# Residual, normalisation, router, routing and scatter of a two-block network: one loop that routes two chunks at a time

## The reference

```python
x = x + _L0_conv_ref(_ln_c(x), ...)     # ends in relu(bn(out) + identity)
t = _to_tokens(x)                       # 6272 tokens of 256 channels
t = t + _L0_ffn_ref(_ln_t(t), router_w, expert_weights)

def _L0_ffn_ref(x, router_w, expert_weights):
    logits = jnp.einsum('bsh,eh->bse', x, router_w)
    rw = jax.nn.softmax(logits, axis=-1).reshape(T, E)
    vals, idx = jax.lax.top_k(rw, TOP_K)            # 2 of 32 experts
    w_masked = jnp.zeros_like(rw).at[jnp.arange(T)[:, None], idx].set(vals)
    def body(acc, we):
        w_e, W_e = we
        return (acc + x_flat * w_e[:, None] @ W_e, None)   # W_e is 256 x 256
```

## Time and profile before

| | us |
|---|---|
| median of 3 runs | 2848.42 |
| lowest and highest | 2834.99, 2849.97 |
| the profiled execution | 2840.76 |
| its span | 2838.9 |

### The profile page before, as it was taken

How to read it: one execution, slowest core, us unless ns; L and a number is a source line. 1 busy time by engine, 2 the same in 40 slices (tenths; PEclk the granted TensorE clock), 3 DMA queues, 4 the chain that set the end, 5 groups by cost and what they waited for, 6 DMA issues and landing times. The chain is left out here.

```text
span 2838.9 us, 36666 instructions
## 1 busy us (share of the span) xinstructions
PE 2048.5 (72%) x12037; PEld 1095.3 (39%) x12038; DVE 1423.7 (50%) x1980; ACT 1257.6 (44%) x1519; POOL 975.0 (34%) x721
## 2 busy tenths in 40 slices
PE   2999279996967300087655578289989999898998
PEld 1454145553535200066522245134434444343444
DVE  3666325553545750022245445358576675856753
ACT  1444112222545100021111134287878888788887
POOL 4332211110000027700076400155555555554554
PEclk9999669997988655599956689699999999999999
DMA  1100122210046144355522111355546555555554
GB/s 27 34 24 12 38 66 60 62 45 5 1 147 221 58 154 127 110 169 172 152 71 64 45 52 68 88 136 145 137 123 161 136 148 143 144 141 133 153 145 114
DMA packets 230098, 286.27 MB, mean 101 GB/s; under 512 B 50612, under 2 KB 186628, under 8 KB 229828
## 3 DMA queue, kind: packets, MB, share of 16 engines
q1 hardware_dynamic: 191268, 233.00, 30.2%
q0 software_dynamic: 12288, 25.72, 3.0%
q10 hardware_dynamic: 26400, 25.70, 2.6%
HBM read 209.00 MB, written 75.25 MB: 100 GB/s over the span
## 5 line engine op out<-in xcount | busy, mean ns | idle before, releaser
L2062 ACT ACTIVATE BIG<-psA,b_s 128x1024 f32<-128x1024 f32 x784 | 811.1, 1115 | 226.3 <-PE psA L2006 226.3
L2006 PE MATMUL psA<-x_r,w_r 128*128 128x512 f32 x1568 | 482.6, 430 | 45.1 <-ACT BIG L2062 28.1
L1995 POOL TENSOR_TENSOR BIG<-BIG 128x1024 f32<-128x1024 f32 x147 | 366.8, 2495 | 381.9 <-DVE BIG L2083 187.3
L2083 DVE SCALAR_TENSOR_TENSOR BIG<-psY,b_s,BIG 128x512 f32<-128x512 f32 x392 | 288.8, 746 | 302.2 <-PE psY L2016 276.9
L2016 PE MATMUL psY<-BIG,w_s 128*32 128x512 f32 x3136 | 396.4, 619 | 10.8 <-DVE BIG L2099 6.5
L2006 PEld LDWEIGHTS psA<-x_r,w_r 128*128 128x128 f32 x1568 | 273.8, 192 | 310.5 <-ACT BIG L2062 227.1
L1405 POOL DMA_INDIRECT gath<-yg_d,idx x128 | 133.3, 1042 | 269.3 <-DVE idx L1416 225.1
L1370 ACT ACTIVATE xv<-ps 128x512 f32<-128x512 f32 x66 | 39.4, 597 | 419.3 <-PE ps L1348 419.3
L1348 PE MATMUL ps<-ident,xv 128*128 128x128 f32 x264 | 40.4, 277 | 224.2 <-DMA xv<-xg_d 224.2
L1316 POOL DMA_INDIRECT xg_d<-xnb,idx x128 | 122.5, 957 | 129.5 <-issue 125.6
L2016 PEld LDWEIGHTS psY<-BIG,w_s 128*32 128x32 f32 x3136 | 81.8, 111 | 216.4 <-issue 130.2
(11 more groups left out here) (341 smaller groups left out, 3097.0 us busy)
## 6 DMA issues: line engine op xcount, KB each, us to landing
BIG<-wt_d SPq DMA_DIRECT2D x784, 128.0 KB, 2.8
xv<-hs_d SPq DMA_DIRECT2D x196, 128.0 KB, 3.1
xg_d<-zeros SPq DMA_DIRECT2D x64, 264.0 KB, 3.7
xv<-xg_d SPq DMA_DIRECT2D x66, 256.0 KB, 3.0
BIG<-ypad_d SPq DMA_DIRECT2D x288, 56.0 KB
xv<-x SPq DMA_DIRECT2D x64, 196.0 KB, 3.1
yg_d<-ex ACTq DMA_DIRECT2D x33, 256.0 KB, 3.3
yg_d<-sq ACTq DMA_DIRECT2D x33, 256.0 KB, 3.3
```

The costliest lines, as they stand in the source:

```text
L1995: eng.tensor_tensor(gacc[:, w % 2], gacc[:, w % 2], gsum[:, a % 2], ALU.add).then_inc(Q["acc"], 1)
L2006: mm = eng.matmul(psA[m % 3][:, b * BLK:(b + 1) * BLK], w1_r[:, m % 16], x_r[:, w % 2, b * BLK:(b + 1) * BLK], start=True, stop=True)
L2062: eng.activation(hid[:, m % 8], psA[m % 3][:], ACT.Gelu, bias=b1_s[:, m % 16:m % 16 + 1]).then_inc(Q["gel"], 1)
L2083: eng.scalar_tensor_tensor(out=dst, in0=psY[use % 2][:], scalar=b2_s[:, g % 4:g % 4 + 1], in1=wb[:, g % 3, b * BLK:(b + 1) * BLK], op0=ALU ...
```

## The change

Setup, loop, routing and scatter become one block. Its loop is written out in full and has 18 slots: 16 chunks and two more (`T + GC`), where `GC` = 2 chunks are a group. In slot s the engines do residual and normalisation of chunk s and transposes and router of chunk s-1; from slot 2 on, an even slot also finds the best two experts for the group before (`best`, `second_best`), and an odd slot gives its rows out (`grow`, `place`, `slots`). Instead of counting all tokens first, tiles are given to experts as the chunks go by: a state `st` of 32 experts (tokens so far, tiles so far, an offset) is updated a group, and new tiles are numbered behind those of earlier groups. Ranks within a group come from matmuls with `before_r` and `ones_r`; small matmuls spread tile counts and rows over the partitions. GpSimd scatters straight from `xnb`, now five buffers, as soon as the slot numbers of the group stand. `xn_d` goes. The zeros for `xg_d` are written by SyncE in the third convolution step, 64 transfers from a part of `ex` that GpSimd fills in the kernel's first block. The expert weights are loaded by SyncE, one transfer an expert, as the columns of `BIG` come free. `EID` is made at the end by one matmul from the table `owned`.

```diff
@@ third convolution step @@
+                @block.sync
+                def _(eng):
+                    eng.wait_ge(s_zero, 1)
+                    for q in range(ZQ):
+                        eng.dma_start(xg_d.ap().rearrange("r c -> (r c)").rearrange("(q p f) -> q p f", q=ZQ, p=128)[q],
+                                      zeros).then_inc(s_zf, 16)
...
@@ the new block, GpSimd @@
+                eng.wait_ge(s_zf, ZQ * 16)
+                for t in range(T):
+                    wait(eng, D["slot"], t // GC + 1)
+                    wait(eng, D["ev"], 2 * (t + 1))
+                    for s in range(NSUB):
+                        for j in range(2):
+                            eng.indirect_dma_start(
+                                xg_d.ap(), bass.IndirectOffsetOnAxis(ap=SLOT[:, t * NSUB + s, j:j + 1], axis=0),
+                                xnb[:, t % XB, s], None).then_inc(d_sc[t % XB], 16)
@@ SyncE @@
+                for t in range(T):
+                    wait(eng, D["x1"], t - 1)
+                    for h in range(2):
+                        eng.dma_start(xs[:, t % 2, h].rearrange("p (b w) -> p b w", b=IMGS), x_v[t, :, h]).then_inc(d_ld[t % 2], 16)
+                    weights(t - 1)
@@ VectorE @@
+                def best(g):
+                    wait(eng, D["lgd"], GC * (g + 1))
+                    wait(eng, D["exp"], g)
+                    step(eng.tensor_reduce(mx[:, 0], lgs, AX.X, ALU.max))
+                    eng.tensor_tensor(dl[:], lgs, many(0), ALU.subtract).then_inc(D["dl"], 1)
...
+                def second_best(g):
...
+                    eng.tensor_tensor(MS[:], MK[:, 0], MK[:, 1], ALU.add).then_inc(D["mask"], 1)
+                def grow(g):
+                    old, new = st[:, g % 2], st[:, (g + 1) % 2]
...
+                    wait(eng, D["tot"], g + 1)
+                    step(eng.tensor_tensor(new[:, 0:1], old[:, 0:1], tot_ps, ALU.add))
...
+                    eng.tensor_scalar(rhs_n[:], before[0:E0, 0:E0], col[:, 2:3], old[:, 1:2], ALU.mult, ALU.add).then_inc(D["rhsn"], 1)
+                def place(g):
+                    wait(eng, D["nb"], g + 1)
...
+                def slots(g):
+                    wait(eng, D["rowv"], g + 1)
+                    wait(eng, D["rank"], g + 1)
+                    step(eng.tensor_tensor(am[:], pos, row(0), ALU.is_ge))
+                    step(eng.tensor_tensor(am[:], am[:], row(1), ALU.mult))
+                    step(eng.tensor_tensor(am[:], am[:], pos, ALU.add))
+                    step(eng.tensor_tensor(MM[:], MK[:], am[:].unsqueeze(1).to_broadcast([SUB, 2, GS, E0]), ALU.mult))
+                    step(eng.tensor_reduce(sl[:], MM[:], AX.X, ALU.add))
+                    eng.tensor_copy(SLOT[:, part].rearrange("p s j -> p j s"), sl[:]).then_inc(D["slot"], 1)
...
+                residual_in(0)
+                for s in range(T + GC):
+                    g, odd = s // GC - 1, s % GC
+                    if s < T:
+                        residual(s)
+                    if s + 1 < T:
+                        residual_in(s + 1)
+                    if odd and g >= 0:
+                        grow(g)
+                    if s < T:
+                        deviation(s)
+                    if odd and g >= 0:
+                        place(g)
+                    if not odd and g >= 0:
+                        best(g)
+                    if s < T:
+                        normalise(s)
+                    if not odd and g >= 0:
+                        second_best(g)
+                    if odd and g >= 0:
+                        slots(g)
@@ TensorE, end of a slot @@
+                    if not odd and g >= 0:
+                        wait(eng, D["mask"], g + 1)
+                        wait(eng, D["slot"], g)
+                        eng.matmul(psP[0:SUB, 0:GS * E0], before_r[:], MS[:].rearrange("p s e -> p (s e)"), start=True, stop=False)
+                        for k in range(GS - 1):
+                            eng.matmul(psP[0:SUB, (k + 1) * E0:GS * E0], ones_r[0:SUB, 0:SUB],
+                                       MS[:, k].unsqueeze(1).to_broadcast([SUB, GS - 1 - k, E0]), start=False, stop=False)
+                        for k in range(GS):
+                            m = eng.matmul(tot_ps, MS[:, k].bitcast(F32), ones_c[0:SUB], start=(k == 0), stop=(k == GS - 1))
+                        m.then_inc(D["tot"], 1)
```

484 lines of the change are left out of this document (233 added, 251 removed).

## The result

The changed kernel takes 2763.1 us, median of four runs (2758.3 to 2767.1), against 2844.9 (2835.0 to 2850.0) of the kernel before on the same chip: a ratio of 0.972, with a 95% interval of 0.968 to 0.975. The forecast was 2739 in a range of 2688 to 2796. So the direction and most of the size came as forecast, 82 us of the 110, and 24 us are missing. The profiled execution took 2758.3 us with a span of 2756.6.

What follows compares the result with a forecast made beforehand. Engines taking turns, then VectorE's routing and GpSimd's 161 us scatter alone, bound the 403 us region. Start, first slots, seven 32.5 us pairs, last pair and scatter end at 1094.7: gain 109.5 us, forecast 2739 us, range 2688 to 2796.

Steps and rivals of the forecast that it cites:

- the last group alone sticks out: Behind the loop: only the last group's 16 indirect DMA issues remain unhidden, 20.2 us.
- The zero transfers are hidden: Stage at 690 to 801 us: the 64 moved zero transfers need 85 of its 111 us and cost nothing.
- The prices of VectorE's steps: Loop slots: 0.42 us for 98x256, 0.68 for 98x512, 0.19 for small steps, reciprocal between 0 and 0.55.
- Rival E: Scatter: a wait holds it until the loop's end, 141 us come back, 2880 us; chance 0.03.
- Rival D: Scatter: VectorE shuts out GpSimd's issues; 2761 us with one instruction's wait an issue, 2918 with two; chance 0.03.
- the last pair: Loop's end: the pair of slots without a chunk takes 15.9 us, to 1071.8.
- no effect in the sum either way: Scatter beside VectorE: 16 issues take 21.5 us by the mean, 32.4 at the longest, which is a pair; costed at nothing.
- under the 204 GB/s of now: Loop's DMA traffic: x, weights and scattered rows, 28 MB in 290 us, stay below the present rate; costed at nothing.
- the pair of 32.5: Loop: an even slot of 14.6 and an odd of 17.9 us, bounds 26.5 and 37.8; seven pairs 227.5.
- The odd slot's clock: TensorE in the loop: 1.2 GHz for the first two steps of a slot, 2.4 GHz for those after.
- rival A: TensorE in the pairs: clock stays at 1.2 GHz, pair 37.8, 37 us more, 2776 us; chance 0.2.
- Rival C: Loop: unseen hand-overs, some 35 small steps a pair at 0.25 us more each, 61 us more, 2800; chance 0.14.

Runs made afterwards that it cites:

- e4: Kernel before the change, with only the 64 zero transfers moved to the third convolution step: 2847.7 us, ratio 1.001 to before.
- e5: Changed kernel with the scatter held back until the last slot numbers are known, so other chunks' rows are scattered (timing only): 2864.3 us, ratio 1.006 to before.
- e8: Changed kernel with one more wait: GpSimd scatters a group's second chunk only when the next group's totals are there: 2718.6 us, ratio 0.958 to before.
- e6: Changed kernel with the scatter as plain DMAs from SP to consecutive rows, GpSimd idle in the loop (timing only): 2692.8 us, ratio 0.949 to before.
- e12: e3 with VectorE's update of the totals put back at the head of the odd slot: 2763.0 us, ratio 0.968 to before.
- e7: Changed kernel with the same 128 indirect DMAs each moving 64 of 256 columns into another tensor (timing only): 2715.0 us, ratio 0.957 to before.
- e10: Changed kernel with the same 128 indirect DMAs each moving 128 of 256 columns into another tensor (timing only): 2758.2 us, ratio 0.967 to before.
- e11: Changed kernel with the expert weight loads held back until the last slot numbers are known: 2752.7 us, ratio 0.965 to before.
- e13: Changed kernel with the odd slot's bookkeeping moved behind the normalisation on VectorE, ScalarE and TensorE: 2769.4 us, ratio 0.973 to before.
- e1: Changed kernel with unused extra matmuls filling TensorE's idle time, 16 in even and 26 in odd slots: 2772.8 us, ratio 0.975 to before.
- e3: Changed kernel reordered, nothing added: next residual ahead of normalisation, bookkeeping in one go, next mean straight behind variance: 2673.7 us, ratio 0.943 to before.
- e2: Changed kernel with transposes and router moved on TensorE to behind the variance of their own chunk: 2764.2 us, ratio 0.971 to before.

## Why the prediction was right, and what it missed

**Right, by its steps.** The overlap comes about and the last group alone sticks out: 20.2 us in the sum, and the last burst runs from 1094.38 to 1114.24, 19.9 us. The zero transfers are hidden, in the stage where I put them and in what they leave behind (e4, 1.001). The prices of VectorE's steps hold: 0.42 us for 98x256, 0.69 for 98x512, 0.20 for the reciprocal whose bounds were 0 and 0.55, 0.18 a small step. The expert stage keeps its length. Rival E is out. Rival D is out in its mechanism: issues take 1054 ns on average, the longest 1947, and GpSimd waits 90.8 us for slot numbers, as the group's row on the page of the kernel after shows:

```profile
L1125 POOL DMA_INDIRECT xg_d<-xnb,SLOT x128 | 135.0, 1054 | 177.8 <-DVE SLOT L1240 90.8 <-issue 86.5 <-ACT xnb L1303 0.3
```

The lock that the Trainium skill describes between VectorE and GpSimd (SBUF — State Buffer, section "Who interferes with whom") can therefore account for no more than 97 ns an issue on top of the 957 of the earlier trace rows, and decides nothing; in e5, where the loop is over before the scatter starts, an issue takes 957 ns again.

**Where the 26 us of the region went.** The start was on time (0.2 us early), slots 0 and 1 were 3.5 us shorter than in the sum (19.6 from residual to residual, forecast 23.1), seven pairs took 250.1 instead of 227.5, the last pair 21.4 instead of 15.9, and the tail 4.6 instead of 2.7: -0.2 - 3.5 + 22.6 + 5.5 + 1.9 = 26.3.

**The step that failed** is the one that gave the scatter no effect on the pair: "no effect in the sum either way", and the bytes "under the 204 GB/s of now". I weighed GpSimd against VectorE and the bytes against the DMA's rate, and never the scatter against TensorE. Without that effect (e8, same work, one wait more) the seven pairs take 214.0 and the last 15.3. So the pair of 32.5 was 1.9 too long by itself, and the interference put 5.2 on top, 36 us over seven pairs and 6 in the last. The two errors have opposite signs, and the forecast owes some of its closeness to that.

**The odd slot's clock.** The forecast took 1.2 GHz for a slot's first two steps and 2.4 after. In e5, e6 and e8 that is what the trace shows: mean 2.98 us, variance 1.56 to 1.58. In the changed kernel the variance of the odd slots takes 2.98 too, which is rival A's picture. But the clock doesn't make the totals late: e8's sixteen passes run at the lower level (1.01 us) and are on time, e12's at the higher (0.67 us) and are up to 10.3 us late. And e8 got the clock back without touching TensorE's work.

**Rival C** (hand-overs that the trace doesn't show) came nearest, for the late semaphores are such hand-overs. It had them spread over 35 small steps at 0.25 us. In fact VectorE's steps follow each other within 0.04 us, and the loss sits in TensorE's completions while a scatter is in flight. The groups of VectorE's idle time show the places; of the kernel after, 850.8 to 1093.9 us:

```profile
L1164 DVE TENSOR_TENSOR xv<-xv,rs 128x784 f32<-128x784 f32 x12 | 11.7, 975 | 46.1 <-ACT rs L1314 44.4 <-issue 1.5
L1159 DVE TENSOR_TENSOR xv<-V,psMO 128x784 f32<-128x784 f32 x12 | 11.6, 969 | 15.7 <-PE psMO L1333 12.2 <-issue 2.5 <-remote 1.0
L1175 DVE TENSOR_REDUCE mx<-psN 98x8 f32<-98x256 f32 x7 | 3.0, 424 | 16.4 <-PE psN L1356 11.3 <-issue 5.0
```

and of e8, 850.8 to 1051.8 us:

```profile
L1166 DVE TENSOR_TENSOR xv<-xv,rs 128x784 f32<-128x784 f32 x12 | 11.7, 974 | 24.4 <-ACT rs L1316 24.2
L1161 DVE TENSOR_TENSOR xv<-V,psMO 128x784 f32<-128x784 f32 x12 | 11.6, 971 | 22.4 <-PE psMO L1335 22.4
L1177 DVE TENSOR_REDUCE mx<-psN 98x8 f32<-98x256 f32 x7 | 3.0, 424 | 13.7 <-PE psN L1358 13.7
```

Ahead of the normalisation VectorE waits 21.7 us longer in the kernel after, ahead of the totals 21.5 (28.6 against 7.1, eight each), ahead of the best two 2.7, and 6.7 less for the mean, part of which now passes while it waits for the totals. That is 39 of the 42 us between the two windows.

**What stays open** is by what means the scatter holds TensorE back. Shown: it needs the scatter's DMAs in flight (e5), and in this kernel it comes with rows of 512 and 1024 bytes and not with 256 (e7, e10); it doesn't need the weight loads (e11), nor VectorE waiting for the totals (e13); the low clock doesn't bring it (e8) and a higher one doesn't cure it (e1, e12); a pause of GpSimd ahead of the totals removes it (e8), and so does the order of e3 without any pause. Why e3's order escapes and e12's doesn't, with the same program on TensorE, isn't explained. Not tested: whether plain DMAs spread over the same 22 us would do it (e6's are gone at 866, 3.7 us ahead of the totals' passes), and whether the loads of x, which stand beside the totals in all these kernels, must be there for it to begin. A queue shared by TensorE and the indirect DMAs would be a guess; no run here shows one. The Trainium skill (SBUF — State Buffer, section "SBUF: two separate sides") says that DMA and compute engines use separate ports, that neither can slow the other, and that TensorE never waits for anyone at its port. In the result the trace disagrees: the same 618 matmuls with the same VectorE work take 243 us beside an unpaced scatter and 201 beside a paced one, and the measurement decides. It may still be right about the port, if TensorE is held elsewhere, in its semaphore updates or in its writes to PSUM; no run here separates these.

## What to carry to other kernels

Before a transfer is costed at nothing because it is hidden, ask who works beside it, and compare every engine's waits with and without it: one run with the transfer held back until the end (e5) tells the price of the overlap that no busy share shows. When a semaphore wait ends with "remote" though its producer's record is over, look at what the other queues are doing at that moment, and try a pause or another order before making the producer faster. And work off the chain from one group's numbers to the next in the order that VectorE has work of its own while it waits; here that was worth about as much (e3 against the changed kernel, 83 us by the ratios) as the whole change (81 us by the same measure).

## What the runs showed of the hardware

TensorE's completions can be seen up to 10.3 us after their records end, in most pairs of e1, e2 and e12 1.6 to 2.3 us behind the end of GpSimd's burst of indirect DMAs, while VectorE's steps keep their length. TensorE's records run ahead of its completions in such a stretch, and can then stop: in one pair of e2 the fifteenth and sixteenth of 16 tiny passes start 1.29 and 0.56 us late. Between rows of 256 and 512 bytes the effect went from none to all of it. In e3, e5, e6, e7 and e8 all waits for the totals are explained by TensorE's records; in the others between one and seven of eight are "remote". SP issues a plain DMA of 98 rows in 0.53 us (16 in 8.43), against 1.26 to 1.36 for an indirect one on GpSimd.
